# A graph layer with experts on one core: closing, routing and dispatch made one stage of seven turns

## The reference, cut to what matters

```python
    xn = _layernorm(x, axis=-1)
    x = x + _L0_gnn_ref(xn, ...) + _L0_mix_ref(xn[None], ...)[0]
    x = x + _L0_ffn_ref(_layernorm(x, axis=-1)[None], ...)[0]

    # in _L0_ffn_ref, with E = 8 experts and K = 2:
    mu = jnp.mean(x, axis=-1, keepdims=True)
    var = jnp.mean(jnp.square(x - mu), axis=-1, keepdims=True)
    xn = (x - mu) * jax.lax.rsqrt(var + EPS) * gamma + beta
    logits = jnp.einsum('bsd,de->bse', xn, Wr) + br
    top_vals, top_idx = jax.lax.top_k(logits, K)
    w = jax.nn.softmax(top_vals, axis=-1)
    for e in range(E):
        h = jax.nn.gelu(jnp.einsum('bsd,dh->bsh', xn, W1[e]) + b1[e], approximate=False)
        y_e = jnp.einsum('bsh,hd->bsd', h, W2[e]) + b2[e]
        y = y + y_e * w_full[..., e, None]
```

## Time and profile before

| | us |
|---|---|
| median of 3 runs | 5051.55 (5050.83 to 5053.5) |
| the profiled execution | 5044.08 |
| its span | 5042.3 |
| start of "fin" | 4100.97 |
| start of routing | 4293.50 |
| start of dispatch | 4324.68 |
| start of the experts | 4479.65 |
| start of the gather ("comb") | 4880.67 |

### The profile page before, as it was taken

How to read it: one execution, slowest core, us unless ns; L and a number is a source line. 1 busy time by engine, 2 the same in 40 slices (tenths; PEclk the granted TensorE clock), 3 DMA queues, 4 the chain that set the end, 5 groups by cost and what they waited for, 6 DMA issues and landing times. The chain is left out here.

```text
span 5042.3 us, 107396 instructions
## 1 busy us (share of the span) xinstructions
PE 4191.8 (83%) x19200; PEld 3376.1 (67%) x19201; DVE 3851.4 (76%) x8465; ACT 2724.1 (54%) x10172; POOL 2738.1 (54%) x2848
## 2 busy tenths in 40 slices
PE   2986999999999999978899999999999943049960
PEld 1555888788778788733688878877877833049960
DVE  3444999999999999955799999999999977202222
ACT  0120677777777777731477777767777741013320
POOL 1011777667667677500677767766767723442235
PEclk9998999999999999999999999999999975579985
DMA  4457877777777777534877777777777723522235
GB/s 85 138 195 225 235 215 215 212 216 215 209 212 216 209 217 216 170 118 143 233 219 215 217 209 215 213 210 212 217 213 214 216 74 104 175 94 70 71 95 152
DMA packets 616287, 920.13 MB, mean 182 GB/s; under 512 B 114501, under 2 KB 477829, under 8 KB 615558
## 3 DMA queue, kind: packets, MB, share of 16 engines
q0 software_dynamic: 154448, 501.87, 34.8%
q1 hardware_dynamic: 378390, 323.25, 22.5%
q10 hardware_dynamic: 82848, 88.64, 4.9%
HBM read 800.89 MB, written 112.53 MB: 181 GB/s over the span
## 5 line engine op out<-in xcount | busy, mean ns | idle before, releaser
L870 POOL DMA_INDIRECT edge_kv<-kvD,edge_ix x1760 | 1821.9, 1035 | 961.9 <-issue 556.5
L909 ACT ACTIVATE edge_w<-edge_vj,edge_ex 128x64 f32<-128x64 f32 x7040 | 1872.0, 340 | 647.3 <-PE edge_pa L950 377.1
L927 PE MATMUL edge_ps<-edge_We,edge_ea 112*128 112x256 f32 x7040 | 1842.4, 384 | 52.3 <-DVE edge_prod L1062 19.0
L927 PEld LDWEIGHTS edge_ps<-edge_We,edge_ea 112*128 112x128 f32 x7040 | 1326.9, 191 | 294.0 <-issue 63.6
L950 PE MATMUL edge_pa<-edge_w,edge_oh 128*128 128x260 f32 x3520 | 1095.5, 393 | 122.2 <-DVE acc L984 94.0
L931 PE MATMUL edge_ps<-acc,edge_oht 128*128 x3520 | 1057.8, 381 | 0.3 <-issue 0.3
L950 PEld LDWEIGHTS edge_pa<-edge_w,edge_oh 128*128 128x128 f32 x3520 | 618.2, 189 | 325.3 <-ACT edge_w L911 165.5
L984 DVE TENSOR_TENSOR acc<-acc,edge_pa 128x260 f32 x1760 | 733.0, 416 | 99.2 <-PE edge_pa L950 46.9
L931 PEld LDWEIGHTS edge_ps<-acc,edge_oht 128*128 128x128 f32 x3520 | 675.0, 192 | 96.5 <-issue 1.7
L1030 DVE TENSOR_TENSOR edge_kj<-edge_kv,edge_ps 128x512 f32<-128x512 f32 x880 | 599.1, 681 | 52.3 <-PE edge_ps L931 23.2
L1062 DVE TENSOR_TENSOR edge_prod<-edge_kj,edge_ps 128x512 f32<-128x512 f32 x880 | 598.9, 681 | 0.0
(11 more groups left out here) (228 smaller groups left out, 3194.7 us busy)
## 6 DMA issues: line engine op xcount, KB each, us to landing
edge_ea<-ea_t_dram SPq DMA_DIRECT2D x1760, 112.0 KB
edge_kb<-relD SPq DMA_DIRECT2D x178, 160.0 KB
edge_kv<-kvD,edge_ix POOLq DMA_INDIRECT x1760
kvD<-nodes_kvs ACTq DMA_DIRECT2D x98, 256.0 KB
exp_xr<-xsD SPq DMA_DIRECT2D x105, 128.0 KB
ysD<-exp_yo ACTq DMA_DIRECT2D x105, 128.0 KB
xsD<-mix_zr POOLq DMA_DIRECT2D x26, 512.0 KB
edge_pen<-penD SPq DMA_DIRECT2D x352, 32.0 KB
```

The costliest lines, as they stand in the source:

```text
L870: nc.gpsimd.indirect_dma_start(out=kv[:, j % HT, :], out_offset=None, in_=g.kvD, in_offset=bass.IndirectOffsetOnAxis(ap=ix[:, h, j % HT:j ...
L909: nc.scalar.activation(w[:, j % 4, h * CA:h * CA + C], vj[:, slot, h * C:(h + 1) * C], ACT.Copy, scale=ex[:, x, h, k:k + 1])
L927: nc.tensor.matmul(ps[:, j % 4, 0:D], ea[:, j % HT, k, :], We[:, k, :], start=(k == 0), stop=(k == 1))
```

## The change

- `finish`, `route` and `dispatch` become one stage, `front`, whose seven turns are written out. Its tile names begin with "fin" as before.
- The two largest logits, the counting and the placing of a turn's seven blocks are done by VectorE in the turn behind (`choose`, `count`, `place`). The counts of the turns before are carried along in column 0 of `B`.
- A row's place is known before the totals are: each expert has a region of CAPT = NB + 1 = 50 tiles in xsD, and a row goes to its expert's region plus its running number (`slot`). A table `trow` with the first row of each of the 105 tiles is made at the end, and so is the sorted place `pos` for the gather.
- GpSimd scatters each turn's seven blocks from SBUF, out of `xn`, as soon as `slot` is there; xnD is gone. It does no gamma and beta.
- The second normalization is ScalarE's (`normed`, into `xn`); gamma and beta are put on the transposed block by ScalarE (`turned`, two instructions), and again in `experts` by VectorE (two instructions in place of a copy).
- SP stores `x1` and loads the skip rows (two turns' worth of buffers), W1, b1, b2 in turn 0 and W2 in turn 2.
- The zero fill of `mix` is gone; SP writes one tile of zeros behind each expert's last row, and eight spare tiles.
- In `experts` SP reads the tile's row from `trow` into a register before each load.

```diff
+    z.CAPT = z.NB + 1
...
-            rows = g.xsD.rearrange("(t p) d -> p t d", p=P)
-            parts = [(k, min(k + 4, z.NE)) for k in range(0, z.NE, 4)]
-            for lo, hi in parts:
-                pool.dma_start(rows[:, lo:hi, :], zr[:, 0:(hi - lo) * D].rearrange("p (t d) -> p t d", d=D)).then_inc(s_zs, 16)
-            pool.wait_ge(s_zs, 16 * len(parts))
...
+            skips(0)
+            skips(1)
+            for i in range(NI):
+                for j in range(UB):
+                    b = i * UB + j
+                    sp.wait_ge(s_x1, b + 1)
+                    sp.dma_start(g.x1D[b * P:(b + 1) * P, :], x1[:, j, :]).then_inc(s_st[j], 16)
+                if i == 0:
+                    for e in range(EX):
+                        sp.dma_start(g.W1[:, e, :, :], a["W1"][e].rearrange("(c p) n -> p c n", p=P)).then_inc(s_big, 16)
...
+                if i == 2:
+                    for e in range(EX):
+                        sp.dma_start(g.W2[:, e, :, :], a["W2"][e].rearrange("(c p) n -> p c n", p=P)).then_inc(s_big, 16)
+                if i + 2 < NI:
+                    skips(i + 2)
...
+            def normed(i, j):
+                if i >= 2:
+                    act.wait_ge(s_sc[i % 2][j], 32 * (i // 2))
+                    act.wait_ge(s_tr, (i - 2) * UB + j + 1)
+                nc.scalar.activation(xn[:, i % 2, j, :], sk[:, i % 2, j, :], ACT.Identity, bias=nb[:, i % 2, j:j + 1],
+                                     scale=rs1[:, i % 2, j:j + 1]).then_inc(s_xn, 1)
...
+                for c in range(2):
+                    ins = nc.scalar.activation(xT[:, b % 4, c, :], pT[:, b % 2, c * P:(c + 1) * P], ACT.Identity,
+                                               bias=bet[:, c:c + 1], scale=gam[:, c:c + 1])
...
+            for i in range(NI):
+                pool.wait_ge(s_pos, i + 1)
+                pool.sem_inc(s_step, 1)
+                for j in range(UB):
+                    for k in range(2):
+                        nc.gpsimd.indirect_dma_start(
+                            out=g.xsD, out_offset=bass.IndirectOffsetOnAxis(ap=slot[:, i * UB + j, k:k + 1].bitcast(U32), axis=0),
+                            in_=xn[:, i % 2, j, :], in_offset=None).then_inc(s_sc[i % 2][j], 16)
...
                     for j in range(UB):
                         ins = nc.vector.bn_aggr(mv[:, o, j, :], stat[:, j, :])
                     ins.then_inc(s_mv, 1)
+                    if i > 0:
+                        (choose, count)[o](i - 1)
                     dve.wait_ge(s_sd, 2 * i + o + 1)
...
+                if i > 0:
+                    place(i - 1)
+            choose(NI - 1)
+            count(NI - 1)
+            place(NI - 1)
...
-                        sp.dma_start(xr[:, j, :], g.xsD[bass.ds(t * P, P), :]).then_inc(s_x[j], 16)
+                        row = table(nc, sp, g.trow[0:1, bass.ds(t, 1)], (EX * z.CAPT + EX - 1) * P)[0]
+                        sp.dma_start(xr[:, j, :], g.xsD[bass.ds(row, P), :]).then_inc(s_x[j], 16)
+            sp.dma_start(gam[:, :], a["gamma_T"]).then_inc(s_gb, 16)
+            sp.dma_start(bet[:, :], a["beta_T"]).then_inc(s_gb, 16)
...
-                nc.vector.tensor_copy(xT[:, j % 2, :], pX[:, j % 2, 0:D]).then_inc(s_xT, 1)
+                for c in range(2):
+                    ins = nc.vector.tensor_scalar(xT[:, j % 2, c * P:(c + 1) * P], pX[:, j % 2, c * P:(c + 1) * P],
+                                                  gam[:, c:c + 1], bet[:, c:c + 1], ALU.mult, ALU.add)
+                ins.then_inc(s_xT, 1)
```

More of the change, by code:

```diff
@@ new lines, in front @@
+        B = st.sb("B", [P, 2, EX, UB + 1])
+        S = st.sb("S", [P, 2, EX, UB + 1])
+        T1 = st.sb("T1", [P, UB, EX])
+        tmp = st.sb("tmp", [P, 2, UB, EX])
+        posf = st.sb("posf", [P, 2, NB])
+        cnt = st.sb("cnt", [P, EX])
+        cnti = st.sb("cnti", [P, EX], I32)
+        zrow = st.sb("zrow", [P, EX], I32)
+        zrf = st.sb("zrf", [P, EX])
+        tl = st.sb("tl", [P, EX])
+        gap = st.sb("gap", [P, EX])
+        end = st.sb("end", [P, EX])
+        ti = st.sb("ti", [P, NE], I32)
@@ new lines, in _ @@
+                if i == 2:
[3 more added lines that the diff above has]
+                    skips(i + 2)
+            sp.wait_ge(s_zr, 1)
+            rows = g.xsD.rearrange("(t p) d -> p t d", p=P)
+            for k in range(EX):
+                sp.dma_start(rows[:, EX * CAPT + k, :], zr[:, :]).then_inc(s_zs, 16)
+            sp.wait_ge(s_pad, 1)
@@ L1135, in _ @@
+            first = table(nc, sp, zrow[0:1, :], (EX * CAPT - 1) * P)
+            for e in range(EX):
+                sp.dma_start(g.xsD[bass.ds(first[e], P), :], zr[:, :]).then_inc(s_zs, 16)
+            sp.wait_ge(s_zs, 32 * EX)
+            sp.wait_ge(s_big, 16 * (2 * EX + 2))
+            for j in range(UB):
+                sp.wait_ge(s_st[j], 16 * NI)
         @block.scalar
@@ L1137, in _ @@
             act.wait_ge(s_eps, 1)
+            act.wait_ge(s_w, 64)
             def deviation(i, o):
@@ L1184, in _ @@
+            for h in range(2):
+                for j in range(UB):
+                    pool.wait_ge(s_sc[h][j], 32 * len(range(h, NI, 2)))
         @block.tensor
@@ L1186, in _, with places @@
             pe.wait_ge(s_w, 64)
-            def body(i):
+            def places(i):
+                pe.wait_ge(s_B, i + 1)
+                need(pe, s_T, i)
+                out = pr[:, 0, 0:EX * UB].rearrange("p (e u) -> p e u", e=EX)
+                nc.tensor.matmul(out, tri[:, :], B[:, i % 2, :, 1:UB + 1], start=True, stop=False)
+                nc.tensor.matmul(out, g.ones[:, :], S[:, i % 2, :, 0:UB], start=False, stop=True).then_inc(s_mm, 1)
+            for i in range(NI):
+                if i > 0:
+                    places(i - 1)
                 for j in range(UB + 1):
@@ L1233, in body @@
+            for i in range(NI):
+                at = g.acc[:, i * UB:(i + 1) * UB, :]
+                linked(nc.vector.tensor_scalar(den[:, :, :], heads(at, "p b (h k) -> p b h k")[:, :, :, C], 1e-16, None, ALU.add))
+                linked(nc.vector.reciprocal(rden[:, :, :], den[:, :, :]))
                 for j in range(UB):
@@ L1727 @@
         lay[n] = np.asarray(inputs["L0_ffn_" + n])
+    for n in ("gamma", "beta"):
+        lay[n + "_T"] = np.ascontiguousarray(lay.pop(n).reshape(2, P).T)
     lay["b1_T"] = np.ascontiguousarray(lay.pop("b1").reshape(EX, HID // P, P).transpose(2, 0, 1))
```

452 lines of the change are left out of this document (190 added, 262 removed).

## The result

The changed kernel takes 4892.72 us (median of 4 runs, 4891.72 to 4901.37) against 5051.19 us beside it: the ratio is 0.9692, with a 95% interval of 0.9678 to 0.9705. It is faster by 158.5 us where 190.5 were forecast.

The account below looks back on a forecast made before the run. Serial stages behind barriers (closing, routing, dispatch, idle: 378.7 us) were the bound. Merged: 16.9 + 6 x 19.8 of turns, 35.3 scatters, 10.55 idle; less 1.6 in the experts, 190.5 us saved: 5051.55 to 4861 us, range 4843 to 4893.

Parts of the forecast that it names:

- 19.8 us: New stage: length of each VectorE turn after the first, 19.1 us of work plus 0.7 for two waits.
- the two places named: VectorE's turn: waits of 0.6 us each, for products before choosing and after the placing products; 0.7 counted for both.
- 19.1 us of work: VectorE's turn without waits: both statistics stretches (8.63 and 5.74), choosing 2.1, counting 1.2, placing 1.0, second deviation 0.45.
- 3.2 us as its bound: VectorE's turn: most that GpSimd's scatters would add if they slowed VectorE as GpSimd's arithmetic did.
- (b): New stage: turns 3.2 us longer through late products or slowed VectorE, 19 us in all, 4880 us; chance 0.12.
- Turn 0: New stage's first turn, without choosing, counting or placing: 16.9 us.
- Scatters: GpSimd in the new stage: each scatter costs 1.27 us, fourteen a turn 17.8 us, so it keeps up.
- (a): New stage: GpSimd becomes the bound with scatters at 1.96 us each, 133 us saved, 4918 us; chance 0.07.
- (c): New stage: each scatter waits out seven two-operand VectorE instructions, 3.7 us each; 37 us slower, 5089 us; chance 0.02.
- the 1.66 us: Edge stage: a GpSimd instruction that met a VectorE one took 1.66 instead of 0.95 us; upper bound 1.96 per scatter.
- From the seventh turn to the last scatter's end: New stage's tail: scatters of block groups 5 and 6 run on end, 28 x 1.27 - 0.3 = 35.3 us.
- (d): New stage: the DRAIN goes or TensorE's half clock is lifted, 12 us more saved, 4849 us; chance 0.06.

Follow-up runs that it names:

- late_again: Changed kernel with all 98 scatters issued after the last turn's placing, from a tile of zeros; 4969.99 us against 5045.11 before.
- w2_early: Changed kernel with W2's eight loads issued in turn 0 instead of turn 2, on chip 9; 4847.75 us against 5033.11 before.
- w2_early_again: Same kernel as w2_early, W2's loads in turn 0 instead of turn 2, on chip 11; 4920.47 us against 5061.68 before.
- after_third: The changed kernel unaltered, measured a third time, on the same chip as after_again; 4897.16 us against 5045.11 before.
- after_again: The changed kernel unaltered, measured once more, beside w2_early_again on chip 11; 4923.08 us against 5061.68 before.
- after_fifth: The changed kernel unaltered, measured again as base for a run with ordered scatter rows; 4930.27 us against 5063.70 before.
- busy_late: Changed kernel with all scatters after the last placing and fourteen GpSimd fills of a scratch tile beside each turn from 1; 4993.74 us against 5067.31.
- more_incs: Changed kernel with 26 more VectorE semaphore updates per turn, around bn_aggr in both statistics; 4934.13 us against 5067.31 before.

## Why the prediction was wrong

- The step that failed: "A turn is then **19.8 us**, below by 0.7 if neither wait comes, above by 3.2 if GpSimd's scatters slow VectorE as its arithmetic did." The sum itself held: where nothing stalls a turn takes 20.1 us (late_again), with waits of 0.42 and 0.62 us at the two places named, so 19.1 us of work as worked out. What failed is the price of the scatters beside the turn, put at nothing with 3.2 us as its bound. The bound was taken from one mechanism, slower long instructions, and these weren't slowed at all. What the scatters delay are the waits at semaphores and the short dependent instructions, by 4 to 10 us a turn. In the first profiled execution the six turns cost 32.1 us more than forecast, in the later ones of the changed kernel up to 49. Why a scatter delays them stays open.
- Rival (b), which had 0.12, has the right sign and place, the wrong cause and 60% of the size: 3.2 us a turn where the first execution lost 5.35. That the measured 4892.7 us stands at the very end of the stated range, 4893, is luck: the range reached so far for (b), whose mechanism didn't act, and the four later medians of the changed kernel, 4897 to 4930 us, lie beyond it.
- Turn 0: 16.9 us, as forecast. Turn 1 waits 1.9 us for pl; no placing stands ahead of it to cover part of the products' time, and I had given it the wait of the others.
- Scatters: 0.971 us and 0.30 between, 1.27 as taken; 98 on end took 125 us (late_again). Rivals (a) and (c) rested on a dearer scatter and have fallen: the 1.66 us that the prediction took from an edge row doesn't come again, and the longest of the 98 took 1.160. The Trainium skill ("SBUF — State Buffer", Who interferes with whom) says that "PE and ACT never wait on anyone"; that is about the ports of the SBUF. ScalarE's 2.95 us above is a wait at a semaphore, so it neither bears that out nor speaks against it.
- From the seventh turn to the last scatter's end: 4321.1 - 4283.2 = 37.9 us where 35.3 were forecast. The DRAIN is 8.065 us, and from the last scatter to the experts it takes 11.3 in place of 10.55. Rival (d) has fallen: TensorE's granted clock stayed at 0.50 throughout the stage.
- The experts: 402.6 us forecast, 402.7 measured (4332.33 to 4734.98), TensorE at 3.76 us a tile. VectorE's two copies take 0.40 us each, not 0.29, and stay hidden.
- The stage, added up: turns +32.1, tail +2.6, barrier +0.7, first den 3.7 us after the stage's start in place of 5.0, -1.3: 34.1 us, which is 220.6 against 186.5. The gather was 2.7 us longer, 164.3 us, where the four later executions of the changed kernel have 160.7 to 162.7 and w2_early 164.1; that is the spread between executions.
- The whole: on chip 9, without stalls, the kernel that differs only in W2's place saved 185.4 us (ratio 0.9631, 0.9612 to 0.9651) of the 190.5. The forecast describes that case; the first comparison and the four later ones of the changed kernel had the stalls.

Was it to be seen ahead? Only as a hint. GpSimd's group of gathers on the page of a kernel lists waits without a cause the page could show ("issue"); w2_early's page, without stalls, and w2_early_again's:

```profile
L861 POOL DMA_INDIRECT edge_kv<-kvD,edge_ix x1760 | 1824.4, 1037 | 934.4 <-issue 446.7
```

```profile
L861 POOL DMA_INDIRECT edge_kv<-kvD,edge_ix x1760 | 1827.5, 1038 | 964.6 <-issue 564.9
```

The two kinds stand apart in every profile: the four of the group without stalls have 428.1 to 447.4 us there, the sixteen others 547.1 to 572.8. The kernel before has 556.5, so it seems to have run on a chip of the stalling kind. The part ahead of the new stage, some 4100 us, ended 25 us later in w2_early_again than in w2_early (first den at 4119.56 and 4094.64), but executions with stalls differ among themselves by as much (4104.49 in after_third, 4127.60 in after_again), so what the hint is worth in time isn't shown.

## What to carry to other kernels

Before you put indirect transfers beside a chain of short dependent instructions, price the waits at semaphores in the chain, and not only the instructions: here the long instructions kept their times and the waits cost 4 to 10 us a turn. When a wait names a releaser that makes no sense, look whether the producer had ended, and repeat the same kernel on another chip before you explain it by the change. Compare variants with the kernel that they vary, on the same chip: a group without it proves nothing.

## What the runs showed that I had not expected

- While GpSimd's indirect scatters are in flight, VectorE's fin_lg starts up to 6.7 us after the last product that it waits for had ended by the profile (after_again and after_fifth, turn 2; 0.04 us in turns 3 to 5 of w2_early), and dependent short instructions follow at 0.7 us in place of 0.2 to 0.3. In one of six groups of runs, the one on chip 9, this didn't happen at all (20.2 against 29.0 us for the same turn). Ordinary stores of the same bytes by SP don't do it.
- A VectorE tensor_scalar of 128x256 floats, with one such input in SBUF and two of one column, that starts beside a GpSimd fill of 128x1040 floats ends 0.15 us after the fill, at 1.13 to 1.18 us in place of 0.40; the tensor_tensor with two such inputs keeps its 0.42 (busy_late).
- Eight sem_inc of VectorE in a row hold up its next instruction by 0.80 us (more_incs).
